# Cross-attention and FFN on one core: maxima head by head, FFN pieces one unit later, transposed halves one by one, attention from two banks in turn

## The reference

```python
xn = layernorm(x)                                        # (512, 512), eps 1e-5
q  = ln32(xn @ Wq + bq) * qn_w + qn_b                    # 16 heads of 32, eps 1e-6
k, v = ln32(ctx @ Wk + bk) * kn_w + kn_b, ctx @ Wv + bv  # the first 496 context rows
kd, vd = ln32(ctx_d @ Wkd + bkd) * ..., ctx_d @ Wvd + bvd  # the last 16 context rows
a  = softmax(q k^T / sqrt(32)) v + softmax(q kd^T / sqrt(32)) vd
x  = x + a @ Wo + bo
h  = silu(layernorm(x) @ lut[gate_idx].T) * (layernorm(x) @ lut[up_idx].T)   # 1376 wide
x  = x + h @ lut[down_idx].T
```

## Time and profile before

| | us |
|---|---|
| median of 3 runs | 897.27 |
| the profiled execution, its own time | 901.39 |
| its span, first to last instruction | 899.5 |
| TensorE busy in the span | 789.3 (88%) |
| VectorE busy | 523.5 (58%) |
| ScalarE busy | 489.1 (54%) |
| GpSimd busy | 234.2 (26%) |
| mean granted TensorE clock | 0.952 of full speed |

### The profile page before, as it was taken

How to read it: one execution, slowest core, us unless ns; L and a number is a source line. 1 busy time by engine, 2 the same in 40 slices (tenths; PEclk the granted TensorE clock), 3 DMA queues, 4 the chain that set the end, 5 groups by cost and what they waited for, 6 DMA issues and landing times.

```text
span 899.5 us, 14490 instructions
## 1 busy us (share of the span) xinstructions
PE 789.3 (88%) x5761; PEld 308.0 (34%) x5761; DVE 523.5 (58%) x938; ACT 489.1 (54%) x961; POOL 234.2 (26%) x250
## 2 busy tenths in 40 slices
PE   3755566699898999999989999999899999979998
PEld 1321122222244333323444333224343332234443
DVE  7758999776673789321737983217368930052220
ACT  2555577686643688565436885653358856611100
POOL 6584100000055322100563222004542210002420
PEclk9985788799999999999999999999899999999999
DMA  8458853356421000121210001312100000000000
GB/s 255 115 149 250 235 151 94 88 137 154 120 66 40 1 1 1 37 70 48 64 44 1 1 1 31 77 41 65 26 1 1 1 25 24 25 23 1 1 10 37
DMA packets 72387, 56.49 MB, mean 63 GB/s; under 512 B 33216, under 2 KB 60352, under 8 KB 72320
## 3 DMA queue, kind: packets, MB, share of 16 engines
q1 hardware_dynamic: 71984, 55.31, 22.4%
q10 hardware_dynamic: 208, 0.26, 0.1%
q0 software_dynamic: 128, 0.00, 0.0%
HBM read 40.67 MB, written 8.45 MB: 55 GB/s over the span
## 4 chain that ended last, share of the span: by engine, by line
PE 49%; DVE 22%; ACT 11%; issue 7%; SPq 3%; DMA 3%; POOL 3%; POOLq 0%; DVEq 0%; ACTq 0%
PE ps L1228 33%; DVE nmax L1035 7%; DVE arena L865 6%; ACT ps L748 5%; PE ps L1434 4%; PE ps L1415 4%; PE ps L1388 4%; ACT arena L774 2%; SPq L399 2%; POOL hrstd L587 2%; DMA arena<-idx 2%; PE ps L1280 2%; SPq L362 2%; PE ps L1421 1%; DVE arena L1036 1%
## 5 line engine op out<-in xcount | busy, mean ns | idle before, releaser
L1228 PE MATMUL ps<-arena,wf_hi 128*128 128x512 f16 (+1 forms) x704 | 216.1, 389 | 12.1 <-DMA arena<-arena 7.8
L748 ACT ACTIVATE ps<-ps,nmax 128x496 f32<-128x496 f32 x256 | 165.2, 646 | 66.9 <-DVE arena L1036 65.7
L774 ACT ACTIVATE arena<-ps 128x1024 f32<-128x1024 f32 x128 | 125.4, 1023 | 75.1 <-PE ps L1421 75.0
L1035 DVE TENSOR_REDUCE nmax<-ps 128x2 f32<-128x992 f32 x128 | 151.6, 1184 | 21.0 <-PE ps L1388 21.0
L1228 PE MATMUL ps<-arena,wf_lo 128*128 128x512 f16 (+1 forms) x352 | 136.2, 387 | 0.0
L587 POOL TENSOR_TENSOR hrstd<-hvar,mhalf 128x16 f32<-128x16 f32 (+1 forms) x33 | 96.7, 2938 | 70.1 <-DVE hvar L949 69.8
L1228 PE MATMUL ps<-wf_hi,arena 128*128 128x512 f16 (+1 forms) x352 | 114.2, 380 | 0.3
L1280 PE MATMUL ps<-arena,wf_lo 128*32 128x512 f16 (+1 forms) x1056 | 81.2, 448 | 26.1 <-ACT wf_lo L658 21.5
L1228 PEld LDWEIGHTS ps<-arena,wf_hi 128*128 128x128 f16 (+1 forms) x704 | 67.1, 102 | 104.4 <-issue 16.2
L865 DVE TENSOR_SCALAR arena<-arena,wf_lo 128x2048 f16<-128x2048 f16 (+1 forms) x132 | 93.8, 769 | 13.8 <-DMA arena<-idx 10.9
L557 POOL TENSOR_TENSOR xrstd<-xvar,mhalf 128x1 f32<-128x1 f32 x32 | 20.4, 637 | 271.0 <-DVE xvar L901 271.0
(11 more groups left out here) (134 smaller groups left out, 974.8 us busy)
## 6 DMA issues: line engine op xcount, KB each, us to landing
arena<-idx SPq DMA_DIRECT2D x124, 128.0 KB, 2.8
arena<-in_x SPq DMA_DIRECT2D x32, 256.0 KB, 3.0
wf_lo<-in_idx SPq DMA_DIRECT2D x10, 512.0 KB, 5.6
out<-arena SPq DMA_DIRECT2D x16, 256.0 KB, 2.0
idx<-wf_hi SPq DMA_DIRECT2D x10, 384.0 KB, 3.3
wf_lo<-in_idx SPq DMA_DIRECT2D x11, 256.0 KB, 6.9
arena<-in_ctxT SPq DMA_DIRECT2D x4, 512.0 KB, 5.1
arena<-in_Wq SPq DMA_DIRECT2D x4, 256.0 KB, 5.1
```

The source lines that it names most:

```text
L748: last = act.activation(sc, sc, ACT.Exp, bias=nmax[:, 0, t, h:h + 1], accum_out=den[:, 0, t, h:h + 1])
L774: act.activation(probs[n_ % 2][:, 2 * p:2 * p + 2, :], ps[:, bank:bank + 2, :], ACT.Exp).then_inc(s["probs_set"], 1)
L1035: dve.tensor_reduce(nmax[:, 0, t, 2 * p:2 * p + 2], sc[:, :, DCA:S], AX_X, ALU.max, negate=True)
L1228: last = pe.matmul(dst, l, r, start=(first and i == 0), stop=(stop and i == len(todo) - 1))
```

## The change

It does four things, the first only in the repetitions.

- The maxima of a pair are taken head by head: the copy of the extra keys comes first, then two reductions over 496 columns, each of which increments `max_set`. ScalarE waits before each exponential for its own head. `max_set` counts to 64 instead of 32 in a core; in batch 0 the pair's copy adds 2 at once.
- The ten FFN pieces of slots 3 to 8 lie in slots 4 to 8, two in each. Tanh, gate product, up product and splitting of tile 0 move by a slot with them.
- In SP's `turn` the high half is transposed as soon as it is there, and only then SP waits for the low half.
- `weigh_values` writes to banks 5 and 4 in turn (`pv_bank`), `attn_hi` comes behind the second exponential, and the waits for `attn_lo` move on by a group.

```diff
@@ -67,7 +67,7 @@
 DOWN_PARTS = ((0, 2), (2, 4), (4, 6), (6, 8), (8, IT))
 PIECES = ([(kind, it, half) for it in range(IT) for kind in ("gate", "up") for half in (0, 1)]
           + [("down", t, part) for t in range(T) for part in range(len(DOWN_PARTS))])
-PER_SLOT = {3: 2, 4: 2, 5: 1, 6: 2, 7: 2, 8: 1}
+PER_SLOT = {4: 2, 5: 2, 6: 2, 7: 2, 8: 2}
 PER_SLOT.update({S_ONE + m: 1 for m in range(NS)})
 PER_SLOT.update({S_SHIFT: 4, S_SHIFT + 1: 2})
 PER_SLOT.update({S_TWO + n_: 1 for n_ in range(G * T)})
@@ -297,6 +297,7 @@
         LB0 = (VB, VB + 1, TB, TB + 1)
         ps16 = lambda bank: ps[:, bank, :].bitcast(F16)
         pair_bank = lambda m: (VB, AB, TB)[m % 3]
+        pv_bank = lambda g: (XB, AB)[g % 2]
         proj_bank = lambda u, first: AB + (BANKS_0 if first else BANKS)[u]
 
 
@@ -389,14 +390,12 @@
             load_rep(1)
             sp.wait_ge(s["wd_lo"], 1)
             sp.dma_start(st_o.rearrange("p (k n) -> p k n", k=G), by_chunk("Wo")).then_inc(s["wo_in"], 16)
-            def staged(kind, t, bt):
-                sp.wait_ge(s[f"hi{kind}"], (nth(bt, T, t + 1)))
-                sp.wait_ge(s[f"st{kind}"], (nth((bt[0], bt[1] - 1) if kind == 1 else bt, T, t + 1)))
-
-            def turn(kind, t):
+            def turn(kind, t, bt):
                 st, dst = (x_st, xT) if kind == 1 else (x2_st, xT2)
-                for i in range(2):
-                    sp.dma_start_transpose(dst[i][:, :, t * P:(t + 1) * P], st[i][t]).then_inc(s[f"xt{kind}"], 16)
+                sp.wait_ge(s[f"hi{kind}"], nth(bt, T, t + 1))
+                sp.dma_start_transpose(dst[0][:, :, t * P:(t + 1) * P], st[0][t]).then_inc(s[f"xt{kind}"], 16)
+                sp.wait_ge(s[f"st{kind}"], nth((bt[0], bt[1] - 1) if kind == 1 else bt, T, t + 1))
+                sp.dma_start_transpose(dst[1][:, :, t * P:(t + 1) * P], st[1][t]).then_inc(s[f"xt{kind}"], 16)
 
             def dca_values(bt):
                 sp.wait_ge(s["v_evac"], nth_value(bt, len(values_of(bt))))
@@ -411,8 +410,7 @@
                 if c == 2:
                     dca_values((0, 0))
                 if c in turn_x:
-                    staged(1, turn_x[c], (0, 1))
-                    turn(1, turn_x[c])
+                    turn(1, turn_x[c], (0, 1))
                 for t in next_x.get(c, ()):
                     if t < 2:
                         sp.wait_ge(s["ps1"], T)
@@ -451,15 +449,13 @@
                 src = [tile_of(flat, (xaddr(b, 2, t))) for t in range(T)]
                 res = residual_row((b + 1))
                 for t in range(T):
-                    staged(2, t, (b, 0))
-                    turn(2, t)
+                    turn(2, t, (b, 0))
                 for t in range(2):
                     load_x(t, src[t], xs[t])
                 dca_values((b, 1))
                 replace(b, 0, res)
                 for t in range(T):
-                    staged(1, t, (b, 2))
-                    turn(1, t)
+                    turn(1, t, (b, 2))
                     if t < 2:
                         load_x(t + 2, src[t + 2], xs[t])
                     if t == 1:
@@ -469,8 +465,7 @@
                 load_context((b + 2), (b * (G * T) + 2 * G * T))
             last = residual_row(B - 1)
             for t in range(T):
-                staged(2, t, (B - 2, 0))
-                turn(2, t)
+                turn(2, t, (B - 2, 0))
             dca_values((B - 1, 0))
             for t in range(T):
                 replace(B - 2, t, last)
@@ -741,9 +736,9 @@
 
                 for m in range(NS):
                     t, p = divmod(m, H // 2)
-                    act.wait_ge(s["max_set"], nth(a, NS, m + 1))
                     for j in range(2):
                         h = 2 * p + j
+                        act.wait_ge(s["max_set"], nth(a, 2 * NS, 2 * m + j + 1))
                         sc = ps[:, pair_bank(m) + j, DCA:S]
                         last = act.activation(sc, sc, ACT.Exp, bias=nmax[:, 0, t, h:h + 1], accum_out=den[:, 0, t, h:h + 1])
                     last.then_inc(s["S_exp"], 1)
@@ -762,7 +757,7 @@
 
                 def attn_hi(g):
                     act.wait_ge(s["pv_done"], nth(a, G * T, T * (g + 1)))
-                    act.activation(aT[0][g], ps[:, AB, :], ACT.Identity, bias=bvs[:, g:g + 1]).then_inc(s["aT_hi"], 1)
+                    act.activation(aT[0][g], ps[:, pv_bank(g), :], ACT.Identity, bias=bvs[:, g:g + 1]).then_inc(s["aT_hi"], 1)
 
                 for n_ in range(G * T):
                     for p in range(2):
@@ -772,7 +767,7 @@
                             act.wait_ge(s["pv_done"], nth(a, G * T, n_ - 1))
                         bank = SC + 2 * p
                         act.activation(probs[n_ % 2][:, 2 * p:2 * p + 2, :], ps[:, bank:bank + 2, :], ACT.Exp).then_inc(s["probs_set"], 1)
-                        if p == 0 and n_ and n_ % T == 0:
+                        if p == 1 and n_ and n_ % T == 0:
                             attn_hi(n_ // T - 1)
                     if nxt is not None and n_ in TURN_AT:
                         stage(1, TURN_AT[n_], nxt)
@@ -972,9 +967,9 @@
 
                 def dca_top(t):
                     if t < T - 1:
-                        dve.wait_ge(s["max_set"], nth(a, NS, (t + 1) * H // 2))
+                        dve.wait_ge(s["max_set"], nth(a, 2 * NS, (t + 1) * H))
                     else:
-                        dve.wait_ge(s["max_set"], nth(a, NS, NS))
+                        dve.wait_ge(s["max_set"], nth(a, 2 * NS, 2 * NS))
                     dve.tensor_reduce(nmax[:, 1, t, :], dca(t), AX_X, ALU.max, negate=True).then_inc(s["dca_max"], 1)
 
                 def dca_shift(t):
@@ -1032,8 +1027,15 @@
                     t, p = divmod(m, H // 2)
                     dve.wait_ge(s["S_done"], nth(a, NS, m + 1))
                     sc = ps[:, pair_bank(m):pair_bank(m) + 2, :]
-                    dve.tensor_reduce(nmax[:, 0, t, 2 * p:2 * p + 2], sc[:, :, DCA:S], AX_X, ALU.max, negate=True)
-                    dve.tensor_copy(sd[:, t * H + 2 * p:t * H + 2 * p + 2, :], sc[:, :, 0:DCA]).then_inc(s["max_set"], 1)
+                    extra = sd[:, t * H + 2 * p:t * H + 2 * p + 2, :]
+                    if prev is None:
+                        dve.tensor_reduce(nmax[:, 0, t, 2 * p:2 * p + 2], sc[:, :, DCA:S], AX_X, ALU.max, negate=True)
+                        dve.tensor_copy(extra, sc[:, :, 0:DCA]).then_inc(s["max_set"], 2)
+                    else:
+                        dve.tensor_copy(extra, sc[:, :, 0:DCA])
+                        dve.tensor_reduce(nmax[:, 0, t, 2 * p:2 * p + 1], sc[:, 0:1, DCA:S], AX_X, ALU.max, negate=True).then_inc(s["max_set"], 1)
+                        dve.tensor_reduce(nmax[:, 0, t, 2 * p + 1:2 * p + 2], sc[:, 1:2, DCA:S], AX_X, ALU.max, negate=True)\
+                           .then_inc(s["max_set"], 1)
                     if m == 1 and prev is not None:
                         low_half(NU - 1)
                     if t and p == 0:
@@ -1065,7 +1067,7 @@
 
                 def attn_lo(g):
                     dve.wait_ge(s["aT_hi"], nth(a, G, g + 1))
-                    dve.scalar_tensor_tensor(out=aT[1][g], in0=ps[:, AB, :], scalar=bvs[:, g:g + 1], in1=aT[0][g],
+                    dve.scalar_tensor_tensor(out=aT[1][g], in0=ps[:, pv_bank(g), :], scalar=bvs[:, g:g + 1], in1=aT[0][g],
                                              op0=ALU.add, op1=ALU.subtract).then_inc(s["aT_lo"], 1)
 
                 for n_ in range(G * T):
@@ -1309,8 +1311,8 @@
                     elif prev is not None and u >= 2:
                         if nth(prev, T, 0):
                             pe.wait_ge(s["down_evac"], nth(prev, T, 0))
-                    elif prev is not None and u == 1:
-                        pe.wait_ge(s["aT_lo"], nth(prev, G, G))
+                    elif prev is not None:
+                        pe.wait_ge(s["aT_lo"], nth(prev, G, G - 1 + u))
                     if kind == "q":
                         pe.wait_ge(*((s["lo1"], t + 1) if prev is None else (s["xt1"], nth(a, 32 * T, 0))))
                         for i in range(KQ):
@@ -1427,11 +1429,11 @@
                     pe.wait_ge(s["probs_set"], nth(a, NR, 2 * n_ + 2))
                     if n_ == 0:
                         pe.wait_ge(s["vd_in"], nth(a, 16, 16))
-                    if kt == 0 and g >= 1:
-                        pe.wait_ge(s["aT_lo"], nth(a, G, g))
+                    if kt == 0 and g >= 2:
+                        pe.wait_ge(s["aT_lo"], nth(a, G, g - 1))
                     for j in range(HG):
                         h = g * HG + j
-                        last = pe.matmul(ps[j * HD:(j + 1) * HD, AB, :], v_sb[:, kt, h * HD:(h + 1) * HD], probs[n_ % 2][:, j, :],
+                        last = pe.matmul(ps[j * HD:(j + 1) * HD, pv_bank(g), :], v_sb[:, kt, h * HD:(h + 1) * HD], probs[n_ % 2][:, j, :],
                                          start=(kt == 0), stop=(kt == T - 1), tile_position=(0, j * HD))
                     last.then_inc(s["pv_done"], 1)
 
```

## The result

The changed kernel takes **872.48 us** (median of 4 runs, 871.29 to 873.71) beside 896.75 us (4 runs, 895.77 to 898.02) for the kernel before on the same chip: a ratio of 0.9729, with a 95% interval of 0.9709 to 0.9748. That is 24.3 us less; 24.0 and 873.3 us were predicted.

The account below looks back on a forecast made before the run. TensorE's pauses and granted clock were taken as the bound. 7.8 + 6.4 + 0.9 + 5.3 + 3.1 + 0.5 = 24.0 us, off the median of 897.27, gave 873.3 us; range 866 to 883.

Parts of the forecast that it names:

- Where the time was: Whole repetitions: TensorE busy 94 to 98% in all three stages, so only its pauses or granted clock can give a gain.
- Pauses and half clock: First stage: transpose waits before the first gate piece 7.8 us, half clock behind them 6.4, last query projection pauses 0.9.
- Rival B: First stage: clock falls anyway or the pause only shrinks; 6.4 us stay, 880 us, or 883 with 1 us pauses; chance 0.12.
- the 1 us in hand: First stage: GpSimd's powers with the normalisation, and the last two head transposes, each finish about 1 us before TensorE needs them.
- rival D: First stage: pauses only change place, to powers and normalisation on GpSimd and VectorE; 890 to 897 us, chance 0.05.
- The turn of halves: First stage, SP's transposes: high half ahead, last issued 1.24 us sooner, landing 2.1 us before TensorE reaches the first gate piece.
- Maxima: Scores stage: head 0's exponential no longer waits for head 1, so the loop shortens; 1.8 us a repetition, 5.3 in three.
- The price of the split: Scores stage, VectorE: a half maximum takes 667 ns, and two halves cost 0.06 us more per pair than one whole.
- the 1.5 us for this term: Scores stage: gain from split maxima if the extra operation costs its whole fixed part, 0.15 us more per pair.
- Rival A: Scores stage: VectorE bounds it because the second reduction's fixed part is not hidden; 877 to 883 us, chance 0.14.
- Two banks: Values stage: alternating banks and later evacuation remove 0.35 us of waiting three times a repetition, 3.1 us in all.
- Batch 0: Stretch before the repetitions: SP issues the first tile's high half without waiting for the low; 0 to 0.75 us, taken 0.5.

## Why the prediction was right

**Where the time was.** That TensorE's pauses and its clock alone bound the repetitions held: each part's gain is a wait or a stretch of half clock that is gone. A wait's row shows less than the wait costs, though, as it counts from the modelled end of the matmul before. The four transposes at 451.48 have a row of 0.60 us, but the next matmul starts 0.44 us behind them where nothing waits. So 0.16 us a wait is missing from the rows of the first stage.

**Pauses and half clock** (7.8 + 6.4 + 0.9 = 15.1 predicted; 15.9 measured over the three first stages). Right, by the step named: the piece comes later than the landing. Undone, the pauses come back. The half clock of the first repetition, taken from the second, was there too: the granted clock is 0.52 from 273.5 to 277. The 0.8 us that the sum had too little are near the 1.0 that its six rows of waits leave out at 0.16 each. But the step that the half clock belongs to *every* such pause is only half right. It followed pauses of 2.08 us and more, and did not follow 1.57 us, twice. Rival B's case (the pause only shrinks and the half clock stays) can't be priced from the length of the pause alone: in two of the three repetitions with the old pieces the shrunk pause kept the clock, and in batch 0 the same 1.97 us did once and once not. So with the old pieces it would have been luck; the change does not rest on it, as it leaves no pause. Nothing is late next: the 1 us in hand that I gave to powers and head transposes was enough, and rival D found no place.

**The turn of halves** was part of that step, as 1.24 us of the 2.1 in hand. Its landing is 1.36 us sooner where the pieces are moved (27.40 us into the second repetition for 28.76), which is the step as I had it. Without moved pieces it cut the pauses only from 2.18, 2.08 and 3.33 to 1.57, 1.57 and 2.35 us. With moved pieces it gives nothing to a repetition, as the landing is 0.9 us or more ahead of gate 0 without it. I counted its lead once, and the sum did not hang on it.

**Maxima** (5.3 predicted; 4.9 by undoing it: 3 x 1.62). The mechanism was right and the size a little high. A repetition gained 1.3 us in the first tile, 0.13 in each of the next two, and 0.13 in the last with what follows it up to the values; the sum was 1.5 + 0.2 + 0.2 - 0.1. The term that was mis-sized is the first tile: 14.07 us, not 13.84, by one wait of 0.18 us for an exponential, because VectorE began 1.34 us behind the scores and not 1.1. I had expected the moved pieces to bring that start forward by 0.3 us; they brought 0.04, since VectorE's gate product stands ahead of the first maxima before and after, and waits for the tanh of a gate piece that TensorE does just ahead of the scores. No run tried the first maxima ahead of that product. The 0.2 of each later tile was rounded up from 14.75 less 14.6. The price of the split was exact: 662 ns against 667, starts 0.58 us apart, 0.06 us a pair.

The prediction gave only half of what the Trainium skill says. Its section (VectorE: DVE Perf Modes, "The DRAIN you can't avoid") goes on that a next operation that is not held starts earlier. The second half maximum does: it starts 0.58 us behind the first, which takes 0.66. So the trace agrees with that sentence, and the 1.5 us for this term rested on the other half alone.

Rival A was right in one thing: VectorE does hold TensorE in the later tiles, though less by the split's price (0.06 us a pair) than by the order of its work, as the run with that work behind the products showed.

**Two banks** (3.1 predicted; 3.5 by undoing it: 3 x 1.18). Right; a little over half is the place behind the second exponential, the rest the bank. The step of the values that held the row of 0.32 us took 3.76 us instead of 3.37: it cost 0.39 us, and I had 0.35.

**Batch 0** (0.5 predicted) is not shown. Its length varies by 7 us between profiles, by 5 with either turn, and a half microsecond is not to be found in that. The 3.4 us between the medians of the run with the old turn and the changed kernel are left open: the intervals of the ratios overlap, and the repetitions are the same.

So that the sum's 24.0 us come this near to the 24.3 measured is partly luck: 0.8 too little in the first stages, 0.4 too much in the maxima, 0.4 too little in the values, and a batch 0 that can cover any of these. The repetitions carry it: 7.35, 7.47 and 9.6 us are 24.4, the third with some 2.2 more in its first stage.

## What to carry to other kernels

When an engine waits for a transfer in the middle of its queue, first look for work of its own that can go ahead: one line of the plan gave 4.6 us a repetition, the split maxima and the second bank 2.8 together. On an engine that feeds the bound one, issue what releases that engine first, and put work that nobody waits for behind it; moving it earlier or later in time, but still ahead of such a release, only changes which release is late. Splitting an operation in two pays where its latency is on the loop, not where its engine is merely busy.

## What the runs showed of the hardware

- In the repetitions the granted clock was down behind the seven idle times of TensorE of 2.08 to 3.33 us, to between 0.65 and 0.50 over the 3 to 5 us behind them, and stayed at 1.00 behind 1.57 us (twice). There 0.51 us less of a pause made the stage 2.20 us shorter. Length alone does not decide: behind the same 1.97 us in batch 0 of two profiles of one kernel it was 0.51 in one and 1.00 in the other.
- The idle time in a row of TensorE is less than the wait costs: 0.16 us less at the waits of the first stage, 0.07 at those of the values.
- VectorE starts the next operation before the end of the last: a reduction of 496 elements a partition takes 662 ns in the rows, and the next starts after 580. Cutting one of 992 (1186 ns) in two cost 0.06 us.
- Batch 0, the stretch with the loads, repeats badly: it ended between 237.5 and 244.6 us in 13 profiles, for a reason that is not shown, while the changed kernel's repetitions agreed within 0.02 us in both its profiles. Comparing lengths of repetitions told changes of 0.2 us apart that medians of whole runs did not.
